# Attention passes of equal width, and one addition moved behind another on VectorE, in a Mamba and gated-attention kernel

## The chip, the core and the metric

The kernel runs on one core of one Trainium2 chip, in one launch. The metric is the device time in microseconds of that launch, from the median of several runs. The engines work in parallel, each on its own queue in program order, and wait for each other by semaphores: TensorE (PE: matmuls, with its weight loads listed as PEld), VectorE (DVE), ScalarE (ACT), GpSimd (POOL) and SyncE (SP, which only issues transfers here).

## The reference

Eight sequences of 512 rows and 256 columns pass a Mamba block and a feed-forward block. The second holds an attention of 16 heads of 64 columns, whose values and outputs go through gated experts (2 chosen of 8); this attention is where the change lies:

```python
def _gate(x, Wsel):
    s = jax.nn.sigmoid(jnp.einsum('bsd,hed->bhse', x, Wsel))
    _, idx = jax.lax.top_k(s, K)
    return s * jax.nn.one_hot(idx, E, dtype=s.dtype).sum(-2)

def _moe_attn(x, Wq, Wk, Wv, Wo, Wsel_v, Wsel_o):
    q = _rope(jnp.einsum('bsd,hdp->bhsp', x, Wq))
    k = _rope(jnp.einsum('bsd,hdp->bhsp', x, Wk))
    v = jnp.einsum('bsd,bhse,hedp->bhsp', x, _gate(x, Wsel_v), Wv)
    att = jax.nn.softmax(jnp.einsum('bhsp,bhtp->bhst', q, k) / np.sqrt(P), axis=-1)
    o = jnp.einsum('bhst,bhtp->bhsp', att, v)
    return jnp.einsum('bhsp,bhse,hepd->bsd', o, _gate(x, Wsel_o), Wo)
```

## The kernel before

Three stages follow each other. Stage A (Mamba, the gates' scores) takes the first third of the time, stage B is the gated attention, stage C the feed-forward part and the norms. Only stage B is changed.

Stage B goes over 8 pairs of heads and, within a pair, over 8 sequences: 64 rounds, numbered `it`. Each engine has its own loop over the rounds, with its order of work written out by hand in a function `batch`; the order between engines is set by semaphores alone. Products are made in three passes from a high and a low part (fp32r) of each operand, so for each operand ScalarE writes the high part (a copy) and VectorE or GpSimd the low part (a subtraction).

A round runs like this. TensorE computes the values and the scores; VectorE gates the values (`vg`), GpSimd sums them over the experts, ScalarE makes the exponentials. Then, for head 0 and again for head 1:

- TensorE transposes the probabilities, four groups of 128 columns, in `turn_probabilities` (line 1114).
- ScalarE copies each group to `probT_high` (line 1245), VectorE subtracts to `probT_low` (`low_probabilities`, line 1368), in the order of the groups.
- `attend` (lines 1124 to 1136) waits for the group's `probT_low` and runs two passes over it into one PSUM bank: the high probabilities against `vv` with 128 columns (high and low values side by side, line 1133), and the low probabilities against the 64 columns of high values (line 1135). For the last group of a head the narrow pass comes first (line 1132).
- The bank then holds the two halves of the head's output in its lower and upper 64 partitions. `move_part` (line 1256) has ScalarE copy one half into `aside`, on the partitions of the other, and `add_parts` (line 1383) has VectorE add both into `oT`.

Between the heads stand `output_gates` (VectorE) and, after the transposes of head 1, four transposes of the output gates (`turn_gates`, line 1121); ScalarE copies them to `gT` (line 1249), and `low_gates` (line 1376) has VectorE subtract in place on 16 partitions that start at partition 64. `spread_gates` (line 1147) spreads the gates over the columns in four pairs of matmuls, with the raw queries and keys of the next round between them. `gate_outputs` (line 1392, four times) multiplies `oT` with the spread gates. ScalarE copies the products to `ogT_high` (line 1267), GpSimd (head 0, line 974) and VectorE (head 1, line 1399) subtract the low part, and `project` (lines 1070 to 1072, eight groups of six matmuls) ends the round on TensorE.

VectorE's order in `batch` around the change is: `low_probabilities` 0 to 3, `output_gates`, one maximum of `tops`, `add_parts(it, 0)`, `low_probabilities` 4 to 7, `low_gates`, `add_parts(it, 1)`, `gate_outputs` 0 and 1. ScalarE's is: high probabilities 0 to 3, `high_x`, `high_values(it, 1)`, `move_part(it, 0)`, high probabilities 4 to 7, `high_gates`, `move_part(it, 1)`, `high_outputs` 0 to 3.

The counters that tie them: `part_moved` rises once for each `move_part`, `oT_done` once for each `add_parts`, `gT_low` for `low_gates`, `og_done` for each `gate_outputs`. `move_part` waits with

```python
act.wait_ge(pv_psum, it * N + h * TT + TT)
act.wait_ge(oT_done, it * 2 + h)
```

so `move_part(it, 1)` starts once `add_parts(it, 0)` has run. `gate_outputs(it, 0)` waits for both additions. `spread_gates(it, 2)` waits for both additions too, `spread_gates(it, 3)` for two `og_done` of the round, and `project(it, j, 0)` for `ogT_low` of GpSimd.

Of the kernel before, what the change touches and what calls it, by code (L numbers as in the profile page):

```python
# [15 lines left out]
F32, F32R = mybir.dt.float32, mybir.dt.float32r  # L16
ALU = mybir.AluOpType
ACT = mybir.ActivationFunctionType
AX = mybir.AxisListType

P = 128
NB, S, D = 8, 512, 256
TT = S // P
# [6 lines left out]
H, E, HP, F = 16, 8, 64, 1024  # L30
# [758 lines left out]
def stage_b(nc, d, const, acc):  # L789
# [6 lines left out]
    with ExitStack() as ctx:  # L796
        def sb(name, shape, dtype=F32):
            return ctx.enter_context(nc.sbuf_tensor(name, shape, dtype))

        def parts(name, shape):  # L800
            return [sb(f"{name}_{part}", shape, F32R) for part in ("high", "low")]

        def sem(name):
            return ctx.enter_context(nc.semaphore(name))

        ps = ctx.enter_context(nc.psum_tensor("ps_b", [P, 8, S], F32))
# [23 lines left out]
        qk_full = sb("qk_full", [P, 2, S])  # L830
# [1 line left out]
        vg = sb("vg", [P, TT, E, HP])  # L832

        v4 = qk_full[:, :, :].rearrange("p a s -> p (a s)").rearrange("p (t e n) -> p t e n", t=TT, e=E // 2)
        oT, aside = sb("oT", [P, S]), sb("aside", [P, S])
        v2 = sb("v2", [P, TT, E // 4, HP])
        v = sb("v", [P, 2, TT, HP])
        vv = sb("vv", [P, 2, TT, 2 * HP], F32R)
        negmax = sb("negmax", [P, TT, 2])
        total = sb("total", [P, 2, TT])  # L840
        share = sb("share", [P, 2, TT])
# [3 lines left out]
        RING = 4  # L845
        probT = parts("probT", [P, RING, S])
# [5 lines left out]
        consts_loaded, consts_done, zero_done = sem("consts_b_loaded"), sem("consts_b_done"), sem("zero_done")  # L852
# [7 lines left out]
        v_high, v_low = sem("v_high"), sem("v_low")  # L860
        s_psum, max_done, exp_done = sem("s_psum"), sem("max_done"), sem("exp_done")
        pT_psum, pT_high, pT_low, pv_psum = sem("pT_psum"), sem("pT_high"), sem("pT_low"), sem("pv_psum")
        gate_step, gT_psum, gT_high, gT_low = sem("gate_step"), sem("gT_psum"), sem("gT_high"), sem("gT_low")
        part_moved, oT_done, spread_psum, og_done = sem("part_moved"), sem("oT_done"), sem("spread_psum"), sem("og_done")
# [11 lines left out]
        ATTEND_BANK = (4, 5)  # L876
# [50 lines left out]
        def turns(eng, start, batch, pair_start=None):  # L927

            def pair(j, more):
                if pair_start:  # L930
                    pair_start(j)
                with eng.Fori(0, NB - 1) as b:
                    batch(j * NB + b, j, b, True, False)
                batch(j * NB + (NB - 1), j, NB - 1, False, more)

            start()
            with eng.Fori(0, PAIRS - 1) as j:
                pair(j, True)
            pair(PAIRS - 1, False)

        @block.gpsimd
        def _(pool):
            def low_x(it):
                pool.wait_ge(xT_high, it + 1)
                pool.tensor_tensor(xT[1][:, :, :], xT_in[:, :, :], xT[0][:, :, :].bitcast(F32), ALU.subtract).then_inc(xT_low, 1)
# [20 lines left out]

            def low_values(it, h):
                pool.wait_ge(v_high, it * 2 + h + 1)
                pool.tensor_tensor(vv[:, h, :, HP:2 * HP], v[:, h, :, :], vv[:, h, :, 0:HP].bitcast(F32), ALU.subtract).then_inc(v_low, 1)

            def low_outputs(it, e):

# [85 lines left out]
                    rank_four(it + 1, ahead)  # L1058

            pool.memset(out_gate[:, :, :], 0.0).then_inc(zero_done, 1)  # L1060
            low_x(0)

            pool.dma_start(acc[:, :, :, :], d["xT"].rearrange("b p k s -> p b k s")).then_inc(acc_loaded, 16)
# [3 lines left out]
        def _(pe):  # L1067
# [56 lines left out]
            def attend(it, h, c):  # L1124

                if c == 0:
                    pe.wait_ge(v_low, it * 2 + h + 1)
                n = h * TT + c
                pe.wait_ge(pT_low, it * N + n + 1)
                bank, last = ATTEND_BANK[h], c == TT - 1  # L1130
                if last:
                    pe.matmul(ps[0:HP, bank, :], vv[:, h, c, 0:HP], probT[1][:, n % RING, :], start=False, stop=False)
                mm = pe.matmul(ps[:, bank, :], vv[:, h, c, :], probT[0][:, n % RING, :], start=(c == 0), stop=last)
                if not last:
                    mm = pe.matmul(ps[0:HP, bank, :], vv[:, h, c, 0:HP], probT[1][:, n % RING, :], start=False, stop=False)
                mm.then_inc(pv_psum, 1)

            def spread_gates(it, p):

# [63 lines left out]
                    project(it, j, n)  # L1203

            pe.wait_ge(consts_done, 1)
            turns(pe, start, batch)

        @block.scalar
        def _(act):
# [26 lines left out]

            def high_values(it, h):
                act.wait_ge(vsum_done, CREDIT + it * VSUM + h * 6 + 6)
                act.activation(vv[:, h, :, 0:HP], v[:, h, :, :], ACT.Copy).then_inc(v_high, 1)

            def high_probabilities(it, n):
                act.wait_ge(pT_psum, it * N + n + 1)
# [74 lines left out]
        def _(dve):  # L1317
# [12 lines left out]
            def rotate(it):  # L1330

                dve.wait_ge(vsum_done, CREDIT + it * VSUM)
                dve.wait_ge(rot_done, it * 3 + 3)
                dve.tensor_tensor(qk_full[:, :, :], rot[:, 0:2, :], rot[:, 2:4, :], ALU.add).then_inc(qk_done, 1)

# [4 lines left out]
            def gate_values(it, j, b, p):  # L1340

                h, at = p // 2, 2 * (p % 2)
                if p == 0:
                    dve.wait_ge(gates_done, it + 1)
                dve.wait_ge(vsum_done, CREDIT + it * VSUM + (at // 2 * 3 + 1 if h else 0))
                dve.wait_ge(v_psum, CREDIT + it * 2 * TT + 2 * p + 2)
                dve.tensor_tensor(vg[:, at:at + 2, :, :], ps[:, PAIR_BANK[p]:PAIR_BANK[p] + 2, :].rearrange("p t (e n) -> p t e n", e=E),  # L1347
                                  gates[:, at:at + 2, h * E:(h + 1) * E].unsqueeze(3).to_broadcast([P, 2, E, HP]),
                                  ALU.mult).then_inc(vg_done, 1)
# [21 lines left out]
            def low_gates(it):  # L1371

                dve.wait_ge(gT_high, it + 1)
                rows = slice(LOW_ROW, LOW_ROW + 2 * E)
                low = gT[rows, :]
                dve.tensor_tensor(low, ps[rows, GT_BANK, :], low.bitcast(F32), ALU.subtract).then_inc(gT_low, 1)

            def add_parts(it, h):

                here = slice(h * HP, (h + 1) * HP)  # L1380
                dve.wait_ge(part_moved, it * 2 + h + 1)
                dve.wait_ge(og_done, CREDIT + it * EP)
                dve.tensor_tensor(oT[here, :], ps[here, ATTEND_BANK[h], :], aside[here, :], ALU.add).then_inc(oT_done, 1)
# [37 lines left out]
            def batch(it, j, b, more, more_pairs):  # L1421
                coming = (it + 1, j if more else j + 1, b + 1 if more else 0)
                gate_values(it, j, b, 0)
                maxima(it, 0)
                maxima(it, 1)
                gate_values(it, j, b, 1)
                maxima(it, 2)
                maxima(it, 3)
                gate_values(it, j, b, 2)
                gate_values(it, j, b, 3)  # L1430
                for n in range(TT):
                    low_probabilities(it, n)
                output_gates(it)
                if more or more_pairs:
                    tops(*coming, 0)
                add_parts(it, 0)
                for n in range(TT, N):
                    low_probabilities(it, n)
                low_gates(it)
                add_parts(it, 1)  # L1440
                gate_outputs(it, 0)
                gate_outputs(it, 1)
                if more or more_pairs:
                    tops(*coming, 1)
                gate_outputs(it, 2)
                gate_outputs(it, 3)
                if more or more_pairs:
                    turn_raw(it + 1)
                low_outputs(it, 0)
                if more or more_pairs:  # L1450
                    swap_halves(it + 1)
                low_outputs(it, 1)
                if more:
                    tops(*coming, 2)
                if more or more_pairs:
                    rotate(it + 1)
                low_outputs(it, 2)
                low_outputs(it, 3)
                if more_pairs:
                    tops(*coming, 2)  # L1460
                    low_qk(it + 1)
                    tops(*coming, 3)
                elif more:
                    tops(*coming, 3)
                    low_qk(it + 1)
                dve.wait_ge(acc_loaded, 16)
                dve.wait_ge(out_psum, CREDIT + it * KD + KD)
                dve.tensor_tensor(acc[:, bass.ds(b, 1), :, :], acc[:, bass.ds(b, 1), :, :], ps[:, OUT:OUT + KD, :].unsqueeze(1),
                                  ALU.add).then_inc(acc_done, 1)

            dve.wait_ge(tables_loaded, 32)
            dve.wait_ge(consts_done, 1)
            dve.wait_ge(zero_done, 1)
            turns(dve, start, batch)


# [394 lines left out]
```

## Time and profile before

| | us |
|---|---|
| median of 3 runs | 4357.75 (4352.01 to 4357.77) |
| profiled execution, whole time | 4360.78 |
| its span, first to last instruction | 4358.8 |
| stage B within the span, from the first fill to the last gates | about 1447 to 4060 |

The profile is one execution. A row of a timeline gives the start in us from the span's start, the duration in us, the engine, the line of the kernel, the operation, the tiles written and read, the shape and how many instructions are merged in the row; in brackets stands how long the engine had been idle and what ended that. Matmuls are pipelined: one of 512 columns is listed with 0.39 us, while the next starts 0.23 us after it. For TensorE, read the distance of starts.

### The profile page before, as it was taken

What the parts mean: (1) busy time and instruction counts of PE and PEld (TensorE: products, weight loads), DVE (VectorE), ACT (ScalarE), POOL (GpSimd) and SP (SyncE); (2) the same over time, 40 slices, a digit from 0 to 9 for tenths busy, and PEclk for the clock granted to TensorE, in tenths of its full rate; (3) what the DMA queues carried; (4) which work ended last, traced back from release to release, by engine and by line L of the source; (5) the groups of instructions that cost most, each with busy time, mean ns of one, the idle gap of its engine ahead of it and who ended that gap; (6) DMA issues with size and microseconds to landing.
All of it is one profiled execution on the core that took longest, in us unless ns stands there. A gap on an engine that the chain in (4) does not pass through costs nothing. (4 is left out here: it accounts for less than half of the span.)

```text
span 4358.8 us, 54031 instructions
## 1 busy us (share of the span) xinstructions
PE 3803.9 (87%) x15744; PEld 2541.1 (58%) x15744; DVE 3630.8 (83%) x4012; ACT 2029.6 (47%) x3761; POOL 2849.6 (65%) x2524
## 2 busy tenths in 40 slices
PE   6777867867765599999999999999999999999787
PEld 2233323323322377777777777777777777777676
DVE  5999999999998478877887887887888788778598
ACT  4544535535443244544444444444444444444433
POOL 2758668567594366766766766766766766766444
PEclk8877877877876799999999999999999999999898
DMA  1000000000000300100100100100100100000101
GB/s 39 0 10 15 24 5 19 24 5 19 15 5 20 131 13 12 41 14 10 41 14 10 41 14 10 41 14 10 41 14 10 41 14 10 20 14 15 31 29 44
DMA packets 48726, 97.83 MB, mean 22 GB/s; under 512 B 3570, under 2 KB 33138, under 8 KB 46228
## 3 DMA queue, kind: packets, MB, share of 16 engines
q1 hardware_dynamic: 47620, 92.94, 6.2%
q0 software_dynamic: 1040, 4.19, 0.2%
q8 instruction: 19, 0.31, 0.0%
q14 instruction: 47, 0.39, 0.0%
HBM read 80.34 MB, written 16.78 MB: 22 GB/s over the span
## 5 line engine op out<-in xcount | busy, mean ns | idle before, releaser
L702 DVE TENSOR_TENSOR_SCAN state<-dA,dBx 128x2048 f32<-128x2048 f32 x128 | 726.8, 5678 | 25.9 <-POOL y_part L289 21.3
L1234 ACT ACTIVATE prob<-ps_b,negmax 128x512 f32<-128x512 f32 x512 | 346.1, 687 | 652.3 <-DVE negmax L1353 652.3
L286 POOL TENSOR_TENSOR state<-state,c_copy 128x1024 f32<-128x1024 f32 x120 | 345.5, 2879 | 374.8 <-DVE state L702 374.8
L1347 DVE TENSOR_TENSOR vg<-ps_b,gates 128x1024 f32<-128x1024 f32 x256 | 313.5, 1224 | 253.1 <-PE ps_b L1072 241.1
L961 POOL TENSOR_TENSOR qk_full<-vg 128x512 f32<-128x512 f32 x256 | 329.0, 1285 | 253.3 <-DVE vg L1347 253.3
L549 ACT ACTIVATE dA<-dt,a_neg 128x511 f32<-128x511 f32 x512 | 326.9, 711 | 323.9 <-DVE state L702 323.7
L974 POOL TENSOR_TENSOR ogT_low<-prob,ogT_high 128x512 fp32r<-128x512 f32 x256 | 324.0, 1295 | 208.9 <-ACT ogT_high L1267 208.9
L372 PE MATMUL ps_a<-xp_high,ident_r 33*128 33x512 f32 x256 | 163.0, 637 | 332.6 <-DVE dBx L692 307.9
L1070 PE MATMUL ps_b<-ogT_high,wo_high 128*128 128x512 f32 x1024 | 413.2, 403 | 11.1 <-DVE ogT_low L1399 10.8
L1070 PE MATMUL ps_b<-wv_high,xT_high 128*128 128x512 f32 x1024 | 414.6, 405 | 0.0
L289 POOL TENSOR_TENSOR y_part<-y_part,state 128x1024 f32<-128x1024 f32 x120 | 403.4, 3362 | 9.4
L1072 PE MATMUL ps_b<-ogT_high,wo_low 128*128 128x512 f32 x1024 | 405.2, 396 | 0.0
L1071 PE MATMUL ps_b<-ogT_low,wo_high 128*128 128x512 f32 x1024 | 402.9, 393 | 0.0
L1071 PE MATMUL ps_b<-wv_low,xT_high 128*128 128x512 f32 x1024 | 401.5, 392 | 0.0
L1072 PE MATMUL ps_b<-wv_high,xT_low 128*128 128x512 f32 x1024 | 399.2, 390 | 0.0
L393 PE MATMUL ps_a<-state,ident 128*128 128x512 f32 x512 | 345.9, 813 | 24.8 <-DVE work L719 22.7
L1353 DVE TENSOR_REDUCE negmax<-ps_b 128x2 f32<-128x1024 f32 x256 | 301.0, 1217 | 62.8 <-PE ps_b L1103 62.8
L372 PEld LDWEIGHTS ps_a<-xp_high,ident_r 33*128 33x128 f32 x256 | 59.0, 231 | 495.5 <-DVE dBx L692 399.0
L1368 DVE TENSOR_TENSOR probT_low<-ps_b,probT_high 128x512 fp32r<-128x512 f32 x512 | 316.4, 677 | 2.3 <-ACT probT_high L1245 2.3
L1245 ACT ACTIVATE probT_high<-ps_b 128x512 fp32r<-128x512 f32 x512 | 264.7, 605 | 61.8 <-PE ps_b L1114 59.7
L692 DVE TENSOR_TENSOR dBx<-du,ps_a 128x2048 f32<-128x2048 f32 x128 | 289.0, 2258 | 1.8 <-PE ps_a L373 1.8
L1267 ACT ACTIVATE ogT_high<-ps_b 128x512 fp32r<-128x512 f32 x256 | 153.1, 598 | 242.0 <-PE ps_b L1072 242.0
(237 smaller groups left out, 9530.9 us busy)
## 6 DMA issues: line engine op xcount, KB each, us to landing
xT<-xT_scratch SPq DMA_DIRECT2D x65, 512.0 KB, 3.3
wv<-in_wv SPq DMA_DIRECT2D x8, 1024.0 KB, 4.9
wo<-in_wo SPq DMA_DIRECT2D x8, 1024.0 KB, 7.0
x_in<-in_x SPq DMA_DIRECT2D x8, 512.0 KB, 4.7
x_a<-in_x SPq DMA_DIRECT2D x8, 512.0 KB, 5.3
x_scratch<-x_a SPq DMA_DIRECT2D x8, 512.0 KB, 2.9
xT_scratch<-x2T SPq DMA_DIRECT2D x8, 512.0 KB, 2.6
scores_scratch<-sg SPq DMA_DIRECT2D x8, 512.0 KB, 3.5
```

The lines of the kernel that those rows point to most:

```text
L286: pool.tensor_tensor(state, state, c, ALU.mult).then_inc(hc_part_done, 1)
L289: pool.tensor_tensor(y[:, :, :], y[:, :, :], state, ALU.add).then_inc(y_part_done, 1)
L393: mm = pe.matmul(ps[:, m, :], ident[:, :], h[n % 2][:, m, :], start=(n == 0), stop=(n == NS - 1))
L549: act.activation(dA[n % 2][:, m, 1:S], dt[par][:, m, 1:S], ACT.Exp, scale=a_neg[:, m, n:n + 1]).then_inc(dA_done, 1)
L702: dve.tensor_tensor_scan(h[n % 2][:, :, :].rearrange("p c s -> p (c s)"), dA[n % 2][:, :, :].rearrange("p c s -> p (c s)"), dBx[n % 2][:, ...
L961: pool.tensor_tensor(v4[:, at, :, :], vg[:, at, 0:4, :], vg[:, at, 4:8, :], ALU.add).then_inc(vsum_done, 1)
L974: pool.tensor_tensor(ogT[1][:, e, :], og[:, e, :], ogT[0][:, e, :].bitcast(F32), ALU.subtract).then_inc(oT_low0, 1)
L1070: pe.matmul(out, left(0), right(0), start=start, stop=False)
L1071: pe.matmul(out, left(0), right(1), start=False, stop=False)
L1072: return pe.matmul(out, left(1), right(0), start=False, stop=stop)
L1234: act.activation(prob[h][:, t, :], ps[:, score_bank(t) + h, :], ACT.Exp, bias=negmax[:, t, h:h + 1], accum_out=total[:, h, t:t + 1]).then_ ...
L1368: dve.tensor_tensor(probT[1][:, n % RING, :], ps[:, n % TT, :], probT[0][:, n % RING, :].bitcast(F32), ALU.subtract).then_inc(pT_low, 1)
```

## The change

`vv` gets a third block of 64 columns that is filled with zeros once at the start of the stage, and holds low values, high values, zeros, in this order. The pass of the high probabilities takes the columns of low and high values, the pass of the low probabilities those of high values and zeros: both are 128 columns wide, in this order for all four groups of a head. `aside` loses its own tile and lives in the second half of `qk_full`. On VectorE `add_parts(it, 0)` goes from its place ahead of `low_probabilities` 4 to 7 to the place behind `low_gates`. TensorE and VectorE wait once for the zeros, and `rotate` waits for the additions of the rounds before. `move_part` is not in the diff.

```diff
-        oT, aside = sb("oT", [P, S]), sb("aside", [P, S])
+        oT, aside = sb("oT", [P, S]), qk_full[:, 1, :]
-        vv = sb("vv", [P, 2, TT, 2 * HP], F32R)
+        vv = sb("vv", [P, 2, TT, 3 * HP], F32R)
...
-                pool.tensor_tensor(vv[:, h, :, HP:2 * HP], v[:, h, :, :], vv[:, h, :, 0:HP].bitcast(F32), ALU.subtract).then_inc(v_low, 1)
+                pool.tensor_tensor(vv[:, h, :, 0:HP], v[:, h, :, :], vv[:, h, :, HP:2 * HP].bitcast(F32), ALU.subtract).then_inc(v_low, 1)
...
+            pool.memset(vv[:, :, :, 2 * HP:3 * HP].bitcast(F32), 0.0).then_inc(zero_done, 1)
...
-                bank, last = ATTEND_BANK[h], c == TT - 1
-                if last:
-                    pe.matmul(ps[0:HP, bank, :], vv[:, h, c, 0:HP], probT[1][:, n % RING, :], start=False, stop=False)
-                mm = pe.matmul(ps[:, bank, :], vv[:, h, c, :], probT[0][:, n % RING, :], start=(c == 0), stop=last)
-                if not last:
-                    mm = pe.matmul(ps[0:HP, bank, :], vv[:, h, c, 0:HP], probT[1][:, n % RING, :], start=False, stop=False)
-                mm.then_inc(pv_psum, 1)
+                bank = ATTEND_BANK[h]
+                pe.matmul(ps[:, bank, :], vv[:, h, c, 0:2 * HP], probT[0][:, n % RING, :], start=(c == 0), stop=False)
+                pe.matmul(ps[:, bank, :], vv[:, h, c, HP:3 * HP], probT[1][:, n % RING, :], start=False, stop=(c == TT - 1)).then_inc(pv_psum, 1)
...
+            pe.wait_ge(zero_done, 2)
...
-                act.activation(vv[:, h, :, 0:HP], v[:, h, :, :], ACT.Copy).then_inc(v_high, 1)
+                act.activation(vv[:, h, :, HP:2 * HP], v[:, h, :, :], ACT.Copy).then_inc(v_high, 1)
...
+                dve.wait_ge(oT_done, it * 2)
...
-                add_parts(it, 0)
                 for n in range(TT, N):
                     low_probabilities(it, n)
                 low_gates(it)
+                add_parts(it, 0)
                 add_parts(it, 1)
...
-            dve.wait_ge(zero_done, 1)
+            dve.wait_ge(zero_done, 2)
```

## Rows read from the trace of the kernel before

**Rows 1.** The page: busy time of the engines, and TensorE's granted clock in 40 slices.

```profile
PE 3803.9 (87%) x15744; PEld 2541.1 (58%) x15744; DVE 3630.8 (83%) x4012; ACT 2029.6 (47%) x3761; POOL 2849.6 (65%) x2524
...
PEclk8877877877876799999999999999999999999898
```

**Rows 2.** Windows, stage B: length, busy us of PE, PEld, DVE, ACT, POOL; PEclk; DMA.

```profile
2000.00:2500.00 500.00, 490.94 (x2362) 364.83 (x2361) 401.36 (x508) 239.91 (x487) 355.56 (x419) 1.00 0.07 24
```

**Rows 3.** Waits, 1400 to 4070 us: who waited for whom, us in all, times, longest.

```profile
PEld ps_b L1133 <- DVE probT_low L1368: 142.2, 382, 1.4
...
DVE oT L1383 <- ACT aside L1256: 104.2, 128, 1.5
...
PEld ps_b L1070 <- DVE ogT_low L1399: 14.2, 8, 2.0
```

**Rows 4.** Timeline, TensorE: first and last attention group of head 0.

```profile
2919.72 0.50 PE L1133 MATMUL ps_b<-probT_high,vv 128*128 128x512 f32 x1 [0.24 <-DVE probT_low L1368]
...
2920.06 0.39 PE L1135 MATMUL ps_b<-probT_low,vv 128*64 128x512 f32 x1
...
2921.51 0.44 PE L1132 MATMUL ps_b<-probT_low,vv 128*64 128x512 f32 x1
...
2921.80 0.39 PE L1133 MATMUL ps_b<-probT_high,vv 128*128 128x512 f32 x1
...
2922.03 1.91 PE L1114 MATMUL ps_b<-ident,prob 128*128 128x128 f32 x16
```

**Rows 5.** Timeline, ScalarE and VectorE: between head 0 and head 1.

```profile
2922.31 0.60 ACT L1256 ACTIVATE aside<-ps_b 64x512 f32<-64x512 f32 x1
2922.93 0.60 ACT L1245 ACTIVATE probT_high<-ps_b 128x512 fp32r<-128x512 f32 x1
...
2923.03 0.68 DVE L1383 TENSOR_TENSOR oT<-ps_b,aside 64x512 f32<-64x512 f32 x1 [0.80 <-ACT aside L1256]
2923.64 2.47 DVE L1368 TENSOR_TENSOR probT_low<-ps_b,probT_high 128x512 fp32r<-128x512 f32 x4
```

**Rows 6.** Timeline, all engines: from low gates to the first projection.

```profile
2926.14 0.69 DVE L1376 TENSOR_TENSOR gT<-ps_b,gT 16x512 fp32r<-16x512 f32 x1
...
2926.45 0.40 PE L1133 MATMUL ps_b<-probT_high,vv 128*128 128x512 f32 x1
...
2926.88 1.20 PE L1147 MATMUL ps_b<-gT,spread 128*128 128x512 f32 x4
2926.96 0.59 ACT L1256 ACTIVATE aside<-ps_b 64x512 f32<-64x512 f32 x1 [1.47 <-PE ps_b L1133]
2927.58 0.69 DVE L1383 TENSOR_TENSOR oT<-ps_b,aside 64x512 f32<-64x512 f32 x1 [0.76 <-ACT aside L1256]
...
2928.31 2.35 DVE L1392 TENSOR_TENSOR prob<-oT,ps_b 128x1024 f32<-128x1024 f32 x2
...
2929.31 0.62 PE L1147 MATMUL ps_b<-gT,spread 128*128 128x512 f32 x2
...
2929.57 0.63 ACT L1267 ACTIVATE ogT_high<-prob 128x512 fp32r<-128x512 f32 x1 [2.02 <-DVE prob L1392]
...
2930.28 1.31 POOL L974 TENSOR_TENSOR ogT_low<-prob,ogT_high 128x512 fp32r<-128x512 f32 x1 [3.24 <-ACT ogT_high L1267]
...
2931.16 0.63 PE L1147 MATMUL ps_b<-gT,spread 128*128 128x512 f32 x2
2931.73 0.47 PE L1070 MATMUL ps_b<-ogT_high,wo_high 128*128 128x512 f32 x1
```

**Rows 7.** Timeline, start of stage B, GpSimd: the zero fill and what follows.

```profile
1447.04 0.52 POOL L1060 MEMSET out_gate<- 128x512 f32 x1 [34.49 <-POOLq L123]
1455.42 2.34 POOL L945 TENSOR_TENSOR xT_low<-xT,xT_high 128x1024 fp32r<-128x1024 f32 x1 [7.85 <-ACT xT_high L1213]
```

**Rows 8.** Timeline, TensorE after its first long wait of stage B.

```profile
1478.36 0.63 PE L1072 MATMUL ps_b<-xT_high,wqk_low 128*128 128x512 f32 x1
1478.79 0.63 PE L1070 MATMUL ps_b<-xT_high,wqk_high 128*128 128x512 f32 x1
```

## The prediction

> **What bounds the kernel now.** I read the page first: PE is busy for 87% of the span, and the granted clock is low in stage A and near full in stage B [rows 1]. A window inside stage B says it more sharply: PE is busy for 490.94 of 500 us, at a granted clock of 1.00, while DVE, ACT and POOL have 100 us or more to spare [rows 2]. So stage B is bound by TensorE's own queue, and a change moves the time only where it moves an instruction of that queue. Then the waits: TensorE waits for few things, and the largest sum is that of the attention passes for `probT_low` of VectorE, 142.2 us over 382 waits; the long ones for `ogT_low` are 8, at the ends of the pairs of heads [rows 3]. The last view is the timeline of one round, read for which wait ends last at three places.
>
> The first place is the attention of a head. VectorE delivers `probT_low` every 0.60 us (four in 2.47 us [rows 5]), and each group's two passes start as it arrives; only what follows the last arrival counts. There the narrow pass starts at 2921.51, the wide one 0.29 us later, the next transposes 0.23 us after that [rows 4].
>
> The second is the hand-over between the heads: ScalarE moves a half at 2922.31 to 2922.91 and only then copies the next probabilities; VectorE adds the halves at 2923.03 and starts `probT_low` of head 1 at 2923.64, as that addition ends [rows 5].
>
> The third carries the forecast. After `low_gates` a chain runs beside TensorE: ScalarE moves the second half, VectorE adds it and gates the outputs, ScalarE copies, GpSimd subtracts, and TensorE's first projection starts at 2931.73, 0.14 us after GpSimd's end (2930.28 + 1.31 = 2931.59) and 0.57 us after the first of the two spread matmuls before it, where 2 x 0.23 would do [rows 6]. So TensorE does wait here, a little, and this chain has **no slack left**: what delays ScalarE's move of the second half delays the first projection, and with it everything that TensorE does after. The spread matmuls ahead of it have some: those at 2929.31 need the addition that ends at 2928.27, about 1 us before, and those at 2931.16 the gating that ends at 2930.66, half a us before [rows 6].
>
> **The change, part by part.** *Width.* A narrow and a wide pass both stream 512 columns of probabilities and are listed with 0.39 us (2920.06 and 2921.80 [rows 4]), so a wider low pass costs nothing as long as its weights are loaded beside the pass before. The first three groups of a head end in a wait for VectorE, which covers a few hundredths either way.
>
> *Order in the last group.* The narrow pass no longer leads. A wide pass after a wait is followed by the next after 0.34 us (2919.72 to 2920.06), a narrow one after 0.29 [rows 4]. So the last group of each head takes 0.05 us longer. For head 1 this is covered: TensorE next waits for `gT_low` anyway (2926.45 + 0.23 = 2926.68, start 2926.88 [rows 6]); without that cover it would be another 3 us in all. For head 0 it delays the transposes and ScalarE's move: **+0.05 us a round**.
>
> *The addition leaves its old place.* The probabilities of head 1 are copied by 2922.93 + 0.60 = 2923.53, and VectorE can follow 0.03 us after ScalarE (2927.55 to 2927.58 [rows 6]), so at 2923.56 instead of 2923.64: **-0.08 us a round** [rows 5]. ScalarE doesn't become late for the next three: its copies take 0.60 us, VectorE's steps 0.67. Together the two terms bring `low_gates` 0.03 us earlier than before.
>
> *The addition at its new place.* Here an unchanged line decides: ScalarE's `move_part(it, 1)` waits until `oT_done` counts the addition of head 0. Before, that addition had been done for 3 us. Now it stands on VectorE behind `low_gates`, and ScalarE waits for it, with `move_part(it, 1)` and all of `high_outputs` queued behind. That VectorE was idle for 0.76 us at this place [rows 6] and the addition takes 0.68 [rows 5] doesn't help: VectorE was idle because it waited for the very move that now waits for VectorE. Step by step: `low_gates` ends at 2926.83. The addition starts next. Its start isn't in the trace of before; from below, VectorE starts an instruction 0.07 us before the end of the last (the four of `probT_low`, 0.60 apart at 0.67 each [rows 5]), from above 0.03 us after it, as `low_gates` does behind the fourth (2923.64 + 2.47 = 2926.11, start 2926.14 [rows 5, 6]). I take the upper one, because that row has the same feature: both steps change between tiles that begin at partition 0 and at partition 64. So 2926.86 to 2927.55. ScalarE follows VectorE by about 0.04 us (the first of two gatings in 2.35 us ends at about 2929.53, ScalarE starts at 2929.57 [rows 6]): 2927.59 instead of 2926.96, which is **+0.63 us a round**. The move, the second addition, gating, copy and subtraction follow as before, all later by this.
>
> The Trainium skill has a rule for the choice just made, on the page "VectorE: DVE Perf Modes", section "Two Vector instructions with no wait between them": an instruction whose input or output starts in another group of 32 partitions than the last one's is held until all earlier ones have finished. By that rule `low_gates` (partition 64) had to be held, and the trace agrees, with 0.03 us after the end against 0.07 before it; the moved addition (partition 0) would be held too. Without the rule the sum below would be 0.10 us a round smaller.
>
> *Sum on the path:* -0.03 + 0.63 = **0.60 us a round**. Is it taken up again before the projection? The spread matmuls at 2929.31 have 1 us and stay hidden. Those at 2931.16 would come about 0.15 us late, but then finish long before GpSimd's part arrives at about 2932.2. Behind the first projection TensorE runs without a wait that this would shorten: the later groups (GpSimd 1.3 us each, TensorE 6 x 0.23 = 1.4), the next round's values and scores, which depend on chains that move along with it. So nothing gives it back: 64 x 0.60 = 38.4 us.
>
> *Parts at nothing.* The second zero fill on GpSimd costs about the 0.52 us of the first and sits in front of an idle time of 7.85 us [rows 7]; were that gone, it would be 0.5 us once. The waits for the zeros end with it. `aside` in `qk_full`: it is written when the sums over experts have read their half (ScalarE has waited for them in `high_values(it, 1)`), and `rotate` waits for additions that VectorE itself did in the round before; no new wait ends late. Their price unhidden would be some 0.03 us a round, a semaphore between engines.
>
> The profiled execution took 4360.78 us, so the same execution changed would take 4360.8 + 38.4 = 4399.2. The median of the runs shown is 3.03 us lower; on it the forecast is 4357.75 + 38.4 = **4396 us**.
>
> **The rivals.**
>
> *The wait is covered (not slower).* If the addition of head 0 delays ScalarE by less than TensorE has in hand, only -0.03 us a round is left: 64 x 0.03 = 2 us, 4356 us. It needs 0.6 us of slack at the first projection; the rows speak against it, with about 0.1 us there and the 0.14 us from GpSimd's end to TensorE's start. A cover in part is likelier than a full one: half of it would give 4377. Chance 0.08, nearly all of it within the bound of no change.
>
> *Faster.* The wait is covered, and the equal widths let TensorE load the wide weights ahead of its wait: then the 0.11 us between 0.34 and the unhindered 0.23 goes for head 0, in place of the loss of 0.05. That is -0.08 - 0.06 = -0.14 us from before's 0.29 for the pair, 64 x 0.14 = 9 us, 4349 us. Against it stands that the first pass of a group shows 0.34 us although its values lay ready since long, and it decides only where the first rival holds too. Chance 0.04.
>
> *VectorE or ScalarE slower at the new place.* After ScalarE's move, VectorE started its addition 0.12 us later for head 0 (2922.91 to 2923.03) and 0.03 later for head 1 [rows 5, 6]. If the second addition, now directly behind the first, takes on the larger figure, it is 0.69 us a round, 44 us, 4402 us. Chance 0.15, on the side of the forecast.
>
> *The clock falls.* TensorE's pause at the first projection grows from about 0.1 us to 0.7. Should the granted clock fall for it, matmuls start 0.43 us apart (1478.36 to 1478.79 [rows 8]) instead of 0.23, and eight such a round would be 1.6 us, 102 us in all: 4498. Against it, waits of up to 2.0 us at the ends of pairs leave windows at 1.00 [rows 2, 3]. Chance 0.02.
>
> **How the numbers follow.** The forecast has 0.71, with its own range from the start of the addition: 0.50 us a round (the earlier start) gives 4390, 0.60 gives 4396. With the third rival the slower cases reach 4402, and a scatter of the medians of 3 to 4 us stands on both sides. The range is 4382 to 4406: this leaves out the covered wait, the faster case and the clock, 0.14 together, and takes in a cover of up to a third of the delay. A difference under 0.2% (9 us) can't be told from none by a measurement of this kernel. Slower by more: 0.71 + 0.15 + 0.02 = 0.88; within: 0.08; faster: 0.04.
>
> **What would show it.** In the changed kernel: the addition of head 0 starts 0.03 us behind `low_gates`; ScalarE's second `aside` starts 0.75 us after the end of `low_gates` instead of 0.13, its idle time ended by `oT` of VectorE; `probT_low` of head 1 starts 0.03 us behind ScalarE's copy; GpSimd's first `ogT_low` and TensorE's first projection come 0.6 us later against `low_gates`; the first projection shows an idle time of about 0.7 us ended by GpSimd; windows of stage B show PE busy for 1.5% less. The prediction is wrong if ScalarE's second `aside` starts within 0.2 us of the end of `low_gates`, or if the rounds stay about 40 us long (a window of 500 us then still holds twelve and a half).

## The result, and the profile after

| | us |
|---|---|
| before, median of 4 runs beside the changed kernel | 4354.90 (4352.01 to 4357.77) |
| changed, median of 4 runs | 4391.96 (4389.99 to 4394.83) |
| ratio, 95% interval | 1.0086 (1.0068 to 1.0103) |
| changed, profiled execution and its span | 4393.82, 4391.7 |

The changed kernel is 37 us slower, where 38 were forecast, and 4392 us lie in the range of 4382 to 4406. The spans of the two profiled executions are 32.9 us apart, but from the first to the last round of stage B alone it is 37.4: `low_gates` runs once a round, so the first and the last of its 64 starts give the length of a round. These are the rows of that instruction, by tile, of before and of after (durations in ns, then the first and last start in us):

```profile
L1376 DVE TENSOR_TENSOR gT<-ps_b,gT x64: 689/689/690, 1512.9 to 4056.0; 16x512 fp32r<-16x512 f32 x64
```

```profile
L1375 DVE TENSOR_TENSOR gT<-ps_b,gT x64: 687/689/690, 1509.8 to 4090.3; 16x512 fp32r<-16x512 f32 x64
```

2543.1 us over 63 rounds are 40.37 us, 2580.5 are 40.96: **+0.59 us a round**. What lies ahead of the first of these starts was 3.1 us shorter in this execution, and what lies behind the last one 1.4 us; why isn't shown. Because a whole run scatters by 5 us, the round is the better measure in what follows; it is taken in the same way from every run, and differences of two rounds are worked out before rounding.

The timeline of the changed kernel, for the same stretch as [rows 4 to 6], VectorE, ScalarE, GpSimd and TensorE (start, duration):

```profile
2939.29 0.50 PE L1132 MATMUL ps_b<-probT_high,vv 128*128 128x512 f32 x1
2939.63 0.40 PE L1133 MATMUL ps_b<-probT_low,vv 128*128 128x512 f32 x1
2939.86 0.60 PE L1115 MATMUL ps_b<-ident,prob 128*128 128x128 f32 x4
...
2940.14 0.59 ACT L1254 ACTIVATE qk_full<-ps_b 64x512 f32<-64x512 f32 x1
2940.76 1.09 ACT L1243 ACTIVATE probT_high<-ps_b 128x512 fp32r<-128x512 f32 x2
...
2941.39 0.69 DVE L1367 TENSOR_TENSOR probT_low<-ps_b,probT_high 128x512 fp32r<-128x512 f32 x1 [1.37 <-ACT probT_high L1243]
...
2943.91 0.69 DVE L1375 TENSOR_TENSOR gT<-ps_b,gT 16x512 fp32r<-16x512 f32 x1
2944.63 0.68 DVE L1382 TENSOR_TENSOR oT<-ps_b,qk_full 64x512 f32<-64x512 f32 x1
...
2944.65 1.20 PE L1144 MATMUL ps_b<-gT,spread 128*128 128x512 f32 x4
...
2945.35 0.59 ACT L1254 ACTIVATE qk_full<-ps_b 64x512 f32<-64x512 f32 x1 [2.03 <-DVE oT L1382]
...
2945.97 0.69 DVE L1382 TENSOR_TENSOR oT<-ps_b,qk_full 64x512 f32<-64x512 f32 x1 [0.66 <-ACT qk_full L1254]
2946.70 2.35 DVE L1391 TENSOR_TENSOR prob<-oT,ps_b 128x1024 f32<-128x1024 f32 x2
...
2948.66 3.79 POOL L974 TENSOR_TENSOR ogT_low<-prob,ogT_high 128x512 fp32r<-128x512 f32 x3 [3.85 <-ACT ogT_high L1265]
...
2949.11 0.73 PE L1144 MATMUL ps_b<-gT,spread 128*128 128x512 f32 x2
...
2950.10 0.47 PE L1071 MATMUL ps_b<-ogT_high,wo_high 128*128 128x512 f32 x1 [0.26 <-POOL ogT_low L974]
```

ScalarE's second move (2945.35) was released by the addition of head 0 (2944.63 + 0.68 = 2945.31), 0.75 us after the end of `low_gates` at 2944.60; before it was 0.13 [rows 6]. From the start of `low_gates` to the first projection are 6.19 us (2943.91 to 2950.10) against 5.59 before (2926.14 to 2931.73 [rows 6]): the 0.60 us of the forecast. The waits of the changed kernel, 1400 to 4100 us, name ScalarE's wait for the addition 64 times, and the cost surfaces where TensorE waits for the gating and for GpSimd's low part:

```profile
ACT qk_full L1254 <- DVE oT L1382: 129.7, 64, 2.1
...
POOL ogT_low L974 <- ACT ogT_high L1265: 246.4, 64, 5.4
```

```profile
PEld ps_b L1144 <- DVE prob L1391: 29.9, 64, 2.1
...
PE ps_b L1071 <- POOL ogT_low L974: 16.8, 64, 0.3
```

In the kernel before, the waits list TensorE's wait for the gating (`prob`) in one round only, and that for this `ogT_low` once, with 0.3 us; now both stand there 64 times. The first projection was released by GpSimd before as well: it starts 0.15 us after the end of `ogT_low` in both kernels (median of the 64 rounds), only the idle time in front of it was too short to be listed. The window of 500 us in stage B shows TensorE busy for 488.28 instead of 490.94 [rows 2], still at a granted clock of 1.00, so the clock didn't fall. That is 0.5% less and not the 1.5% that I had said: a matmul is listed with 0.39 us though the next could start after 0.23, so the listing hides 0.16 us of every pause. There are two pauses now, ahead of the spread matmuls at 2949.11 and of the projection, and of the 0.60 us only 0.02 (2948.70 + 0.39 to 2949.11) and 0.26 are listed as idle. For the same reason the projection shows 0.26 us and not the 0.7 us of the prediction's list of signs. By the starts the three parts are 0.18 us (2948.93 to 2949.11), 0.11 us (the two spread matmuls 0.34 instead of 0.23 us apart) and 0.42 us (2949.68 to 2950.10), 0.71 us in all where it was 0.11 before.

```profile
2000.00:2500.00 500.00, 488.28 (x2329) 363.13 (x2329) 396.09 (x500) 237.34 (x483) 347.52 (x410) 1.00 0.07 25
```

### The profile page after: what moved, and what is told of

It is laid out like the page before. It is cut to its first block and busy times, and to the rows that moved or that the text cites. A ratio compares the mean times of both kernels' runs of the same rounds, so it can differ in the third digit from the quotient of the medians.

```text
span 4391.7 us, 54096 instructions
## 1 busy us (share of the span) xinstructions
PE 3829.3 (87%) x15744; PEld 2566.8 (58%) x15744; DVE 3635.1 (83%) x4012; ACT 2029.6 (46%) x3761; POOL 2850.8 (65%) x2525
## 5 line engine op out<-in xcount | busy, mean ns | idle before, releaser
L1132 PE MATMUL ps_b<-probT_high,vv 128*128 128x512 f32 x512 | 255.4, 499 | 22.3 <-DVE probT_low L1367 21.5
```

## The experiments

The ratio of each run is to the kernel before as it was measured beside that run.

Theory **W** is that of the prediction: ScalarE's wait for the moved addition is the delay. Theory **D**: two additions behind `low_gates` make VectorE's way to the gating longer, whoever waits. Theory **C**: the wide passes cost TensorE the time; the page could be read so, as PE's busy time rose from 3803.9 [rows 1] to 3829.3 us.

**1. The wait lifted.**

```diff
-                act.wait_ge(oT_done, it * 2 + h)
+                act.wait_ge(oT_done, it * 2)
```

> The changed kernel, with one thing different: move_part waits for oT_done it * 2 for both heads, so ScalarE's second move no longer waits for the addition of head 0 (the two heads use different partitions of aside). Theory W (the delay is this wait): ScalarE's second move starts 0.13 us behind low_gates again, the addition of head 0 fills VectorE's idle time in front of the second addition (0.03 + 0.69 us of the 0.75 us there), the round keeps only -0.03 us against before, so about 64 x 0.03 = 2 us under before, ratio 0.9995. Theory D (two additions in a row make VectorE's chain to the gating longer, whoever waits): the time stays near the changed kernel's, ratio 1.008. Theory C (the wide passes cost TensorE the time): it stays as well, 1.008.

Measured: 4359.99 us, ratio 1.0009 (1.0000 to 1.0018), a round of 40.42 us ((4055.6 - 1509.0) / 63), +0.06 us against before. One wait holds all but 0.06 of the 0.59 us: W stands, and D and C fall as causes of the delay. Yet 0.09 us a round of what W expected is missing (+0.06 for -0.03). The timeline of this run shows where:

```profile
2923.99 0.69 DVE L1375 TENSOR_TENSOR gT<-ps_b,gT 16x512 fp32r<-16x512 f32 x1
2924.71 1.41 DVE L1382 TENSOR_TENSOR oT<-ps_b,qk_full 64x512 f32<-64x512 f32 x2
...
2924.78 0.59 ACT L1254 ACTIVATE qk_full<-ps_b 64x512 f32<-64x512 f32 x1 [1.38 <-PE ps_b L1133]
...
2927.49 0.63 ACT L1265 ACTIVATE ogT_high<-prob 128x512 fp32r<-128x512 f32 x1 [2.11 <-DVE prob L1391]
```

The addition of head 0 fits in front of the second but for 0.02 us: the second starts 0.05 us after the move's end, where it was 0.03. But ScalarE was idle for 2.11 us between the move's end (2925.37) and its copy of the gated outputs, where it had been 2.02 [rows 6], and the move itself had ended no later (0.69 us after `low_gates`, 0.72 before). Behind the gating's end the copy now starts after 0.11 us (before: 0.03). Runs 6 and 8 take this up.

**2. Only the move.** The kernel before, with the one line moved and nothing else:

```diff
-                add_parts(it, 0)
                 for n in range(TT, N):
                     low_probabilities(it, n)
                 low_gates(it)
+                add_parts(it, 0)
                 add_parts(it, 1)
```

> The kernel before, with only the addition of head 0 moved behind low_gates on VectorE: narrow passes, their order and aside as before. Theory W: 0.63 us a round from the wait, -0.08 from the freed VectorE, nothing for the width: 0.55 us x 64 = 35 us slower, ratio 1.0081; without the wide pass in front the last group of head 0 keeps its 0.28 us. Theory D: the same figure, told apart by the first run. Theory C (the width costs it): ratio 1.000.

Measured: 4390.88 us, 1.0084 (1.0070 to 1.0098), a round of 40.91 us, +0.55, as expected. The move alone makes the delay.

**3. Only the width.** The changed kernel with that line back in its old place.

```diff
+                add_parts(it, 0)
                 for n in range(TT, N):
                     low_probabilities(it, n)
                 low_gates(it)
-                add_parts(it, 0)
                 add_parts(it, 1)
```

> The changed kernel, with the addition of head 0 put back in its old place: only the equal widths, their order, the zeros and aside in qk_full are left. Theories W and D: +0.05 us a round, from the last group of head 0 that takes 0.33 instead of 0.28 us, 3 us slower, ratio 1.0008. Theory C: 1.008. If ScalarE's move of head 0 has some slack against the transposes, less than 3 us.

Measured: 4361.75 us, 1.0014 (1.0005 to 1.0023), a round of 40.45 us, +0.08 instead of +0.05. The last group costs 0.05 us in head 1 too: not to TensorE, which waits for `gT_low` anyway, but to ScalarE's second move, which starts 0.18 us after the end of `low_gates` instead of 0.13 (median of the rounds) and whose chain sets the first projection. I had looked for the cover on TensorE only. In the changed kernel it doesn't show, since there the same move waits for the addition.

**4. Narrow passes, moved and lifted:** run 2 with the edit of run 1.

> The kernel before, with the addition of head 0 moved behind low_gates and move_part waiting for oT_done it * 2 for both heads: the order of the second run without its wait, and the narrow pass first in the last group. Theory W: -0.08 us a round, 64 x 0.08 = 5 us faster than before, ratio 0.9988, the fastest of all. Theory D: 1.008. If VectorE's addition no longer fits in front of the second one (0.72 of 0.75 us), a few hundredths of the gain go.

Measured: 4358.40 us, 1.0006 (0.9997 to 1.0015), a round of 40.39 us: +0.02, not -0.08. It falls short by 0.1 us, much as run 1 does, so the width isn't needed for it. The two rows of the move and the additions show a part of it:

```profile
2925.39 1.41 DVE L1383 TENSOR_TENSOR oT<-ps_b,aside 64x512 f32<-64x512 f32 x2
```

```profile
2925.41 0.59 ACT L1256 ACTIVATE aside<-ps_b 64x512 f32<-64x512 f32 x1 [1.33 <-PE ps_b L1133]
```

The second addition ends at 2926.80, so it starts at about 2926.11, 0.1 us after the move's end at 2926.00 instead of 0.03. This is what is left of theory D: the second addition waits for the first, and with it goes the 0.08 us that the move had gained (it starts 0.05 us behind `low_gates` instead of 0.13). The gating's end and ScalarE's copy are 0.11 us apart here too.

**5. The addition ahead of `low_gates`.** The changed kernel with

```diff
-                low_gates(it)
                 add_parts(it, 0)
+                low_gates(it)
                 add_parts(it, 1)
```

> The changed kernel, with the addition of head 0 one place earlier on VectorE: behind the last probT_low and ahead of low_gates. ScalarE's wait for it is then met (the addition ends 0.2 us before ScalarE is free to move), but low_gates is 0.62 us later and TensorE's spread matmuls wait for it. Theory W, drawn out (VectorE has no idle time for 0.69 us anywhere between the last probT_low and the gating that isn't on one of two chains): low_gates +0.59, first projection +0.5 us a round after 0.09 us of TensorE's slack, 32 us slower than before, ratio 1.0073, and the idle time stands in front of the spread matmuls, not of the projection. If only the place behind low_gates is bad, the ratio is 1.000 to 1.001.

Measured: 4376.99 us, 1.0052 (1.0037 to 1.0068), a round of 40.73 us, +0.37. That is less than the +0.5 forecast, but far from none, and the wait has gone to the spread matmuls:

```profile
2934.74 1.28 DVE L1367 TENSOR_TENSOR probT_low<-ps_b,probT_high 128x512 fp32r<-128x512 f32 x2
2935.94 0.67 DVE L1382 TENSOR_TENSOR oT<-ps_b,qk_full 64x512 f32<-64x512 f32 x1
2936.64 0.69 DVE L1375 TENSOR_TENSOR gT<-ps_b,gT 16x512 fp32r<-16x512 f32 x1
...
2937.38 1.20 PE L1144 MATMUL ps_b<-gT,spread 128*128 128x512 f32 x4 [0.58 <-DVE gT L1375]
...
2941.66 0.63 PE L1144 MATMUL ps_b<-gT,spread 128*128 128x512 f32 x2
2942.13 0.40 PE L1071 MATMUL ps_b<-ogT_high,wo_high 128*128 128x512 f32 x1
2942.36 0.40 PE L1072 MATMUL ps_b<-ogT_low,wo_high 128*128 128x512 f32 x1
```

The first projection follows the second spread matmul (2941.66 + 0.23 = 2941.89) after 0.24 us: TensorE doesn't wait there any more. Its second matmul also starts after 0.23 us instead of 0.31 in the kernel before (2931.73 to 2932.04), which is one part of the 0.13 us that the forecast missed. The waits of TensorE for `ogT_low` at the ends of the pairs are shorter as well, 11.2 against 14.2 us in all [rows 3]; with about 0.08 and 0.05 us a round (3.0 us over 64) the two are as large as the difference. Why the ends of the pairs are shorter isn't shown.

```profile
PEld ps_b L1144 <- DVE gT L1375: 64.6, 64, 1.0
...
PEld ps_b L1071 <- DVE ogT_low L1398: 11.2, 7, 1.6
```

The rows give the start that the forecast had to choose. Behind `probT_low` (2934.74 + 1.28 = 2936.02, both at partition 0) the addition starts at 2935.94, 0.08 us before the end; `low_gates`, at partition 64, starts 0.03 us after the end of the addition (2936.61).

**6. The order of waits.** The kernel before, with

```diff
-                act.wait_ge(pv_psum, it * N + h * TT + TT)
                 act.wait_ge(oT_done, it * 2 + h)
+                act.wait_ge(pv_psum, it * N + h * TT + TT)
...
-                act.wait_ge(og_done, CREDIT + it * EP + n // 2 + 1)
                 if n == 0:
                     act.wait_ge(out_psum, CREDIT + it * KD)
-                elif n >= EP:
+                act.wait_ge(og_done, CREDIT + it * EP + n // 2 + 1)
+                if n >= EP:
...
-                dve.wait_ge(part_moved, it * 2 + h + 1)
                 dve.wait_ge(og_done, CREDIT + it * EP)
+                dve.wait_ge(part_moved, it * 2 + h + 1)
```

> The kernel before, with only the order of waits changed, so that the counter that comes last is waited for last: in move_part oT_done before pv_psum, in add_parts og_done before part_moved, in high_outputs out_psum before og_done. Theory Q (a wait followed by another whose value has to be worked out is paid on the register instruction, about 0.08 to 0.1 us after the event, the last wait rides on the instruction itself, 0.03 us after it): ScalarE's two moves start 0.08 us earlier behind TensorE, VectorE's addition of head 0 0.1 us earlier behind ScalarE, so probT_low of head 1 0.16 and the second addition 0.24 us earlier; TensorE's spread and projection then follow: -0.2 us a round, 64 x 0.2 = 13 us faster than before, ratio 0.997. If the split of the waits isn't set by their order: 1.000.

Measured: 4355.60 us, 1.0002 (0.9993 to 1.0011), a round of 40.33 us, -0.04. A miss in size. The addition of head 0 did start 0.03 instead of 0.12 us after ScalarE's move, but on ScalarE the wait put last went into a semaphore instruction of its own, ahead of the activation, whenever no register had to be worked out between the two. From the gating's end to ScalarE's first copy this took 0.09 us, where it is 0.03 with the wait on the instruction itself and 0.11 with a register instruction in between (run 1); of two waits, it is the first that rides on what follows. This is read from the instructions of the engines' sequencers, which the trace keeps with the semaphore that each waits for, though no view lists them. In the kernel before, ScalarE's first copy carries the wait for `og_done` itself, and that for `out_psum` stands in an EVENT_SEMAPHORE long before it; in run 1 the wait for `og_done` is on an ALU_OP at 2927.407, between the gating's end (2927.375) and the copy (2927.487); in run 6 it is on an EVENT_SEMAPHORE at 2928.499, between 2928.467 and 2928.561.

**7. Moved, lifted, ordered:** run 4 with the edits of run 6.

> The kernel before, with the addition of head 0 behind low_gates, move_part waiting for oT_done it * 2 only, and the same order of waits as in the last one. Theory Q: probT_low of head 1 0.16 us earlier, but the second addition can't start before 0.75 us behind low_gates, as the first one is in front of it (0.03 + 0.68 + 0.03); -0.17 us a round, 64 x 0.17 = 11 us faster than before, ratio 0.9975, a little behind the one without the move. So the move is worth nothing even without its wait.

Measured: 4355.40 us, 1.0002 (0.9993 to 1.0011), a round of 40.34 us, -0.03: the same miss.

**8. Only the order in `high_outputs`,** in run 4.

> The kernel before, with the addition behind low_gates, the wait of move_part lifted and only high_outputs waiting for out_psum before og_done. It isolates why the lifted kernels fell short: there ScalarE's first ogT_high started 0.11 us after the gating's end instead of 0.03. Theory Q: 0.03 again, so 0.07 us a round less than the lifted kernel with narrow passes (20 ns a round over before): -0.05 us a round, 3 us faster than before, ratio 0.9993. If the 0.08 us has another cause (contention of ScalarE and VectorE at PSUM), it stays at 1.0005.

Measured: 4353.56 us, 0.9999 (0.9990 to 1.0008), a round of 40.35 us, 0.04 less than run 4. The idle time in front of ScalarE's first copy of gated outputs, in the timelines of runs 4 and 8:

```profile
2928.17 1.16 ACT L1267 ACTIVATE ogT_high<-prob 128x512 fp32r<-128x512 f32 x2 [2.17 <-DVE prob L1392]
```

```profile
2924.47 0.63 ACT L1266 ACTIVATE ogT_high<-prob 128x512 fp32r<-128x512 f32 x1 [2.15 <-DVE prob L1391]
```

The order matters, by 0.02 us in this place: a semaphore instruction instead of a register instruction. The other 0.02 us lie elsewhere in the round and aren't followed up. What it takes to get the 0.03 us shows in the next run.

**9. One wait for each.** The kernel before, with the waits that are met long before put once at the start of a round:

```diff
-                act.wait_ge(oT_done, it * 2 + h)
...
-                if n == 0:
-                    act.wait_ge(out_psum, CREDIT + it * KD)
-                elif n >= EP:
+                if n >= EP:
...
                 exps(it, 0)
+                act.wait_ge(oT_done, it * 2)
+                act.wait_ge(out_psum, CREDIT + it * KD)
...
-                dve.wait_ge(og_done, CREDIT + it * EP)
...
                 gate_values(it, j, b, 0)
+                dve.wait_ge(og_done, CREDIT + it * EP)
```

> The kernel before, with the waits that are met long before taken out of move_part, add_parts and high_outputs and put once, early in the round (oT_done it * 2 and out_psum on ScalarE, og_done on VectorE), so that each of the three has one wait, for the counter that comes last. The last run showed that of two waits the one written first rides on the instruction (0.03 us from event to start), and that it is paid on a register or semaphore instruction instead (0.06 to 0.12 us) when the other stands between. Expected: ScalarE's two moves 0.08 us earlier behind TensorE, VectorE's addition of head 0 0.1 us earlier behind ScalarE, probT_low of head 1 0.16 us earlier, the second addition 0.24 us earlier, first ogT_high 0.03 us behind the gating; -0.2 to -0.24 us a round, 13 to 16 us faster than before, ratio 0.9965. If only one of two places gains (TensorE's spread matmuls or the projection), -0.16.

Measured: 4348.24 us against 4357.38 beside it, 0.9981 (0.9972 to 0.9990), a round of 40.20 us, -0.17. It beats both kernels. The timeline, to be read beside [rows 5, 6]:

```profile
2914.31 0.42 ACT L1239 ACTIVATE vv<-v 128x256 fp32r<-128x256 f32 x1 [0.63 <-POOL v L965]
2914.76 0.60 ACT L1255 ACTIVATE aside<-ps_b 64x512 f32<-64x512 f32 x1
...
2915.39 0.68 DVE L1381 TENSOR_TENSOR oT<-ps_b,aside 64x512 f32<-64x512 f32 x1 [0.68 <-ACT aside L1255]
2916.01 2.48 DVE L1367 TENSOR_TENSOR probT_low<-ps_b,probT_high 128x512 fp32r<-128x512 f32 x4
...
2918.52 0.69 DVE L1375 TENSOR_TENSOR gT<-ps_b,gT 16x512 fp32r<-16x512 f32 x1
...
2919.26 0.59 ACT L1255 ACTIVATE aside<-ps_b 64x512 f32<-64x512 f32 x1 [1.32 <-PE ps_b L1133]
...
2920.61 1.22 DVE L1390 TENSOR_TENSOR prob<-oT,ps_b 128x1024 f32<-128x1024 f32 x1
...
2921.87 0.63 ACT L1264 ACTIVATE ogT_high<-prob 128x512 fp32r<-128x512 f32 x1 [2.02 <-DVE prob L1390]
```

The addition starts 0.03 us after ScalarE's move (0.12 before), the second move 0.05 us after `low_gates` (0.13 before), and the first copy of gated outputs 0.04 us after the gating's end (2920.61 + 1.22 = 2921.83): the 0.09 and 0.11 us of the runs before came from the waits. It falls short of the -0.2 to -0.24 because ScalarE's first move gained next to nothing: the copy of the values in front of it ends at 2914.73, 0.03 us before it.

**10. The same, with the addition moved.**

> The last one, with the addition of head 0 moved behind low_gates as well (the wait of ScalarE for it is no longer there). This is what the move is worth when nothing hides it. The second addition can't start before 0.75 us behind low_gates, against about 0.67 without the move, and head 1's probT_low gains nothing from VectorE any more, as ScalarE's copy is last there in both: 0.08 us a round slower than the last one, 5 us, ratio to the kernel before 0.9975.

Measured: 4351.81 us, 0.9988 (0.9979 to 0.9997), a round of 40.29 us: 0.09 us a round and 3.6 us slower than run 9, where 0.08 and 5 were expected. With every hindrance gone the move still costs: it puts 0.72 us in front of the second addition, which starts 0.07 us later behind ScalarE's move than in run 9 (0.10 against 0.03, medians), and frees nothing, as VectorE has to wait for ScalarE's copy in either place.

## Why the prediction was right

Point by point, a round, forecast and measured:

- Last group of head 0: +0.05. Measured 0.34 instead of 0.29 us from pass to pass (2939.29 to 2939.63, before 2921.51 to 2921.80). Right.
- The freed place on VectorE: -0.08. ScalarE's copy starts at 2940.76, `probT_low` at 2941.39, 0.63 us later instead of 0.71 [rows 5]. Right. Of the 0.03 us that the two terms leave, only 0.01 reached `low_gates`: from the first `probT_low` of head 1 to `low_gates` it took 2.52 us (2941.39 to 2943.91) instead of 2.50.
- Start of the moved addition: 0.03 us after the end of `low_gates`, the upper of the two ends. Measured 2944.60 to 2944.63. The rule of the Trainium skill, page "VectorE: DVE Perf Modes", section "Two Vector instructions with no wait between them", holds here, and run 5 and the changed kernel show both of its cases with the same instruction.
- The wait: +0.63. ScalarE's move is 0.75 instead of 0.13 us behind `low_gates`, +0.62. Right, and lifted alone it gives 0.54 of 0.59 us back (run 1).
- No cover behind it: the first projection comes 0.60 us later against `low_gates`, the round is 0.59 us longer. Right.
- The late spread matmuls: forecast about 0.15 us late and without effect. They start 0.18 us late and 0.34 us apart instead of 0.23, and the projection waits for GpSimd all the same. Right.

So the sum holds because its parts do, and two small errors (-0.03 us up to `low_gates` where -0.01 came, +0.63 from there to the projection where +0.60 came) nearly cancelled in it, by luck. Two steps beside the sum were wrong. The cover of head 1's last group was claimed for TensorE and forgotten for ScalarE (run 3: 0.08 instead of 0.05). And the rival "covered wait" was priced at -0.03 us, where lifting the wait gave +0.06 (run 1): the sum took the distance from event to start as fixed for each pair of instructions, while it changes with how the waits are split. Neither entered the changed kernel: there the second move waits for the addition, which ends later than the passes of head 1, and both this wait and the copy's wait for the gating are on the instruction itself, 0.03 to 0.04 us behind the event. Two of the signs were of little use as well: PE's busy share and idle time, for the reason given with the window, and the rounds of "about 40 us", since a round of 40.96 us puts 12.2 of them into 500 us where it was 12.4. VectorE had 99 us to spare in the window and not 100 or more. That the agreement is within 1 us of 37 is more than the method gives: the runs of one kernel scatter by 5.

What stays open: run 9 gained 0.17 us a round, 10.4 us over the rounds, and its profiled execution is 19 us shorter than that of before. The other 9 us lie outside the rounds (the first `low_gates` starts 2 us earlier, and what follows the last one is nearly 7 us shorter) and are not explained by the edit. The profiled execution was the fastest of its 11; the medians are 9 us apart, which the rounds account for.

## What to carry to other kernels

Before an instruction is moved past others on one engine, look up every counter that it raises, and for each of its waiters ask whether the wait was met long before: an idle time on the engine that receives it is no room if it ends with an event that now waits for the moved instruction. Where two chains leave one point (here gates and halves behind the last probabilities), a step of 0.7 us has a place only where neither is waiting; the old place, under a copy that VectorE had to wait for anyway, cost 0.08 us, and nothing once the addition followed its move after 0.03 us (run 9). In this kernel it paid to let an instruction on the critical chain wait for one counter alone, and to put waits that are met anyway earlier in the round.

## What was not expected of the hardware

- From the end of the releasing instruction to the start of the one that waits for it, on ScalarE and VectorE, there were 0.03 us when that wait was on the instruction itself, 0.09 when it stood as a semaphore instruction in front, and 0.11 to 0.13 when it was on a register instruction (runs 1, 6 and 9, and the kernel before). Which of these a wait gets follows from its neighbour in the queue: two such places (the addition of head 0 and the second move) made up the 0.17 us of run 9.
- The same addition on VectorE starts 0.08 us before the end of its forerunner or 0.03 us after it, depending on whether both begin at the same partition (run 5 and the changed kernel).
